# Routing a batch two batches behind instead of three, with its work at the end of the attention's steps

## What is computed

```
x = x + attn_a(layernorm(x), Mq, Mk, Mv)        # 8 heads, key size 64, value size 16
x = x + ffn(layernorm(x), w_gate, ...)          # 8 experts, hidden 512, one expert a token
x = x + attn_b(layernorm(x), wq, w_down, ...)   # 16 heads of 8, rotary, paged mask
x = x + ffn(layernorm(x), w_gate, ...)          # the same FFN again
```

```
probs = softmax(x @ w_gate + b_gate); route_p = max(probs); route_idx = argmax(probs)
y = relu(x @ W1[e] + b1[e]) @ W2[e] + b2[e]     # for e = route_idx of the token
out = y * route_p
```

## Time and profile before

| | before |
|---|---|
| median of three runs | 572.63 us |
| profiled execution | 575.24 us |
| its span | 573.4 us |
| mean granted clock | 0.857 |
| TensorE matmul busy | 423.3 us (74%) |
| VectorE busy | 324.9 us (57%) |
| ScalarE busy | 211.7 us (37%) |
| GpSimd busy | 202.3 us (35%) |
| the chain that ended last: TensorE, VectorE, issue | 56%, 15%, 8% |

### The profile page before, as it was taken

The page is one execution under the profiler, slowest core; times in us unless marked ns, Lnnn a source line. Parts: engine busy times, 40 slices in busy tenths (PEclk is TensorE's granted clock), DMA queues, the critical chain, the costliest instruction groups (busy, mean ns, idle before and its releaser), DMA issues.

```text
span 573.4 us, 14608 instructions
## 1 busy us (share of the span) xinstructions
PE 423.3 (74%) x4870; PEld 315.7 (55%) x4871; DVE 324.9 (57%) x1042; ACT 211.7 (37%) x483; POOL 202.3 (35%) x299
## 2 busy tenths in 40 slices
PE   2768878788872599955467899999888763999900
PEld 2646666666662377743135666766666652677800
DVE  2555656775666445426865576668776664444412
ACT  1445645544530022211135657655665400222200
POOL 3132335443445100027666335633612442000054
PEclk9968989998775699995567999999999955899965
DMA  8999200000000111111100000000000001111123
GB/s 271 348 337 296 83 2 13 11 5 5 10 11 27 29 55 53 50 38 37 27 0 2 1 2 3 0 0 0 1 2 10 29 19 32 39 53 54 41 70 90
DMA packets 40896, 30.91 MB, mean 54 GB/s; under 512 B 3344, under 2 KB 37008, under 8 KB 40592
## 3 DMA queue, kind: packets, MB, share of 16 engines
q1 hardware_dynamic: 32176, 23.06, 13.2%
q0 software_dynamic: 2048, 4.20, 2.5%
q10 hardware_dynamic: 6624, 3.02, 1.8%
HBM read 15.26 MB, written 15.01 MB: 53 GB/s over the span
## 4 chain that ended last, share of the span: by engine, by line
PE 56%; DVE 15%; issue 8%; POOL 7%; ACT 7%; DMA 4%; SPq 1%; ACTq 0%; DVEq 0%; POOLq 0%
PE S L1311 8%; PE bank L1324 7%; PE bank L1194 6%; POOL yg L1042 4%; PE S L1317 4%; PE S L1235 3%; PE S L1401 3%; ACT E L910 3%; PE bank L1354 3%; PE S L1402 2%; PE bank L1211 2%; DVE nmax L491 2%; PE bank L1414 2%; PE bank L1377 2%; PE bank L1154 2%
## 5 line engine op out<-in xcount | busy, mean ns | idle before, releaser
L829 ACT ACTIVATE E<-S,nmax 128x256 f32<-128x256 f32 x128 | 59.1, 478 | 59.7 <-DVE nmax L491 59.7
L1042 POOL DMA_INDIRECT yg<-slots,pos x32 | 30.8, 963 | 141.3 <-DMA slots<-yo 132.8
L872 ACT ACTIVATE hT<-S 128x512 f32<-128x512 f32 x46 | 27.5, 597 | 106.6 <-PE S L1317 106.6
L1003 POOL TENSOR_TENSOR vs<-Va,rden 128x512 f32<-128x512 f32 x32 | 33.3, 1040 | 80.1 <-DVE rden L520 77.2
L910 ACT ACTIVATE E<-S 128x1536 f32<-128x1536 f32 x32 | 46.4, 1450 | 25.7 <-PE S L1405 25.7
L1311 PE MATMUL S<-W,xgT 128*128 x92 | 52.3, 652 | 0.0
L677 DVE TENSOR_REDUCE nm<-bank 128x2 f32<-128x512 f32 x64 | 41.1, 684 | 16.1 <-PE bank L1377 16.1
L491 DVE TENSOR_REDUCE nmax<-S 128x4 f32<-128x1024 f32 x32 | 39.1, 1221 | 17.6 <-PE S L1235 16.6
L1324 PE MATMUL bank<-W,hT 128*128 x368 | 48.5, 276 | 0.0
L1324 PEld LDWEIGHTS bank<-W,hT 128*128 128x128 f32 x368 | 44.7, 192 | 0.1
L1148 PE MATMUL bank<-cst,xnb 128*128 128x128 f32 x44 | 11.9, 369 | 40.5 <-DVE xnb L415 29.6
(11 more groups left out here) (169 smaller groups left out, 1010.8 us busy)
## 6 DMA issues: line engine op xcount, KB each, us to landing
slots<-zeros SPq DMA_DIRECT2D x1, 8640.0 KB, 38.0
xg<-slots SPq DMA_DIRECT2D x46, 64.0 KB, 1.8
slots<-yo ACTq DMA_DIRECT2D x46, 64.0 KB, 1.6
W<-in_L_ffn_W SPq DMA_DIRECT2D x1, 2048.0 KB, 10.5
b<-in_L_ffn_b SPq DMA_DIRECT2D x1, 2048.0 KB, 20.1
x<-in_L_attn_a_x SPq DMA_DIRECT2D x4, 256.0 KB, 3.6
yg<-in_select SPq DMA_DIRECT2D x1, 1024.0 KB, 8.1
out<-x SPq DMA_DIRECT2D x8, 128.0 KB, 2.2
```

The lines of the kernel that those rows point to most:

```text
L829: last = act.activation(E[:, hp, h, c, :], S[hp % 2][:, h, c * T:(c + 1) * T], ACT.Exp, bias=nmax[:, hp, k:k + 1], accum_out=den[:, hp, k: ...
L1042: pool.indirect_dma_start(out=yg[:, t, :], out_offset=None, in_=xs_dram, in_offset=bass.IndirectOffsetOnAxis(pos[:, t:t + 1], 0)).then_inc ...
```

## The change

The router in the first attention runs one batch closer behind. Batch b now carries, of batch b-1, the statistics (step 2) and the norm's write, transpose and copy (step 3); of batch b-2, logits (step 0), ranks and places (step 1), and the scatter (step 2). On TensorE the router's instructions stand at the end of a step, behind projection and values. Batch 2 routes for the first time, so the gate's weights `wg` and `bg` count into a semaphore of their own group, waited for at batch 2. The tail is shorter by one batch and in another order. On GpSimd the zeroing of `keys` stands behind a wait for the expert table. In each FFN the first tile's product with W1 precedes the second tile's transpose.

```diff
@@ SyncE: loads
-            sp.dma_start(wg[:, :], wg_in).then_inc(w_loaded, 16)
-            sp.dma_start(bg[:, :], bg_in.unsqueeze(0).to_broadcast([P, NE])).then_inc(w_loaded, 16)
+            sp.dma_start(wg[:, :], wg_in).then_inc(b_loaded, 16)
+            sp.dma_start(bg[:, :], bg_in.unsqueeze(0).to_broadcast([P, NE])).then_inc(b_loaded, 16)
@@ VectorE: a_step
-                if hp == 0 and there(b - 3):
-                    route_logits(0, b - 3, 1 - p, pb[3])
-                if hp == 1:
-                    if there(b - 3): route_places(0, b - 3, 1 - p, pb[3])
-                if hp == 2:
-                    if there(b - 1): dve.wait_ge(a_x, b)
-                    if there(b - 2): norm_apply(1, b - 2, p)
-                    if there(b - 1):
-                        norm_stats(1, b - 1, 1 - p)
+                if hp == 0 and there(b - 2):
+                    route_logits(0, b - 2, p, pb[3])
+                if hp == 1 and there(b - 2):
+                    route_places(0, b - 2, p, pb[3])
+                if hp == 2 and there(b - 1):
+                    dve.wait_ge(a_x, b)
+                    dve.sem_inc(norm[1]["go"], 1)
+                    norm_stats(1, b - 1, 1 - p)
+                if hp == 3 and there(b - 1):
+                    norm_apply(1, b - 1, 1 - p)
@@ VectorE: tail
             a_recip(31, 3)
-            norm_apply(1, 6, 0)
             a_outT(30, 2)
-            route_logits(0, 5, 1, pb[3])
+            route_logits(0, 6, 0, pb[3])
             a_outT(31, 3)
-            route_places(0, 5, 1, pb[3])
             a_add(7, pb[0])
             dve.wait_ge(a_x, 8)
             norm_stats(1, 7, 1)
-            route_logits(0, 6, 0, pb[3])
+            route_places(0, 6, 0, pb[3])
             norm_apply(1, 7, 1)
-            route_places(0, 6, 0, pb[3])
             route_logits(0, 7, 1, pb[3])
             route_places(0, 7, 1, pb[3])
@@ ScalarE: a_step and tail
-                if hp == 3 and there(b - 2):
-                    norm_out(1, b - 2, p, pb[3])
+                if hp == 3 and there(b - 1):
+                    norm_out(1, b - 1, 1 - p, pb[3])
-            norm_out(1, 6, 0, pb[1])
@@ GpSimd: a_batch and tail
-                    if hp == 1 and there(b - 3):
-                        scatter(0, b - 3, 1 - p)
                     if hp == 2 and there(b - 1):
                         inverse_deviation(1, b - 1, 1 - p)
+                    if hp == (3 if isinstance(b, int) and b == 2 else 2) and there(b - 2):
+                        if isinstance(b, int) and b == 2:
+                            pool.wait_ge(slots_zero, 16)
+                        scatter(0, b - 2, p)
...
-            scatter(0, 5, 1)
             inverse_deviation(1, 7, 1)
             scatter(0, 6, 0)
             scatter(0, 7, 1)
+            pool.wait_ge(ffn[0]["table"], 1)
+            pool.memset(sofar[:, :], 0.0).then_inc(pool_const, 1)
             pool.wait_ge(a_scores, 4 * B)
             pool.memset(keys[:, :], 0.0).then_inc(bs["zero"], 1)
-            pool.wait_ge(ffn[0]["totals"], 1)
-            pool.memset(sofar[:, :], 0.0).then_inc(pool_const, 1)
@@ TensorE: a_step
                 last.then_inc(a_scores, 1)
-                if hp == 0 and there(b - 3): logits(0, b - 3, 1 - p, pb[3])
-                if hp == 1 and there(b - 3): ranks(0, b - 3, pb[3])
-                if hp == 3 and there(b - 2):
-                    pe.wait_ge(a_x, b)
-                    norm_transpose(1, b - 2, p, pb[3])
                 if nxt and hp < 3:
                     a_project(b + 1, 1 - p, hp, True)
                 if hp == 2 and lag:
-                    if there(b - 3):
-                        pe.wait_ge(ffn[0]["pos"], b - 2)
+                    if there(b - 2):
+                        pe.wait_ge(ffn[0]["pos"], b - 1)
...
                     a_values_out(g - 2, (hp + 2) % 4)
+                if hp == 0 and there(b - 2): logits(0, b - 2, p, pb[3])
+                if hp == 1 and there(b - 2): ranks(0, b - 2, pb[3])
+                if hp == 3 and there(b - 1):
+                    pe.wait_ge(a_x, b)
+                    norm_transpose(1, b - 1, 1 - p, pb[3])
@@ TensorE: tail
             a_values_out(30, 2)
-            logits(0, 5, 1, pb[3])
-            norm_transpose(1, 6, 0, pb[1])
+            logits(0, 6, 0, pb[3])
             pe.wait_ge(a_ot, 31)
             a_values_out(31, 3)
-            ranks(0, 5, pb[3])
             a_final(7, pb[0])
-            pe.wait_ge(ffn[0]["pos"], 6)
-            logits(0, 6, 0, pb[3])
             ranks(0, 6, pb[3])
-            pe.wait_ge(norm[1]["xnT"], 7)
             norm_transpose(1, 7, 1, pb[1])
@@ TensorE: ffn_tiles (fetch is the wait for tile s+1 and its transpose)
-                    if live(s + 1):
+                    first = isinstance(s, int) and s == 0
+                    if live(s + 1) and not first:
+                        fetch()
                     if live(s):
                         ...
+                    if first:
+                        fetch()
```

More of the change, by code:

```diff
@@ L535, in _ @@
             for b in range(3):
+                if b == 2:
+                    dve.wait_ge(b_loaded, 112)
                 for hp in range(4):
                     a_step(b, hp, b % 2, b > 0, True)
-            dve.wait_ge(w_loaded, 96)
+            dve.wait_ge(w_loaded, 64)
             with dve.Fori(0, 2) as h:
@@ L1016, in a_batch @@
                     a_values(b * 4 + hp, hp, p, lag)
-                    if hp == 1 and there(b - 3):
-                        scatter(0, b - 3, 1 - p)
                     if hp == 2 and there(b - 1):
                         inverse_deviation(1, b - 1, 1 - p)
+                    if hp == (3 if isinstance(b, int) and b == 2 else 2) and there(b - 2):
+                        if isinstance(b, int) and b == 2:
+                            pool.wait_ge(slots_zero, 16)
+                        scatter(0, b - 2, p)
             for b in range(3):
                 a_batch(b, b % 2, b > 0, True)
-            pool.wait_ge(slots_zero, 16)
             with pool.Fori(0, 2) as h:
@@ L1262, in _ @@
             for b in range(3):
+                if b == 2:
+                    pe.wait_ge(b_loaded, 112)
                 for hp in range(4):
                     a_step(b, hp, b % 2, b > 0, True)
-            pe.wait_ge(w_loaded, 96)
+            pe.wait_ge(w_loaded, 64)
             with pe.Fori(0, 2) as h:
@@ L1300, in step, with fetch @@
                         e = pe.value_load(expert[0:1, bass.ds(s, 1)], min_val=0, max_val=NE - 1)
-                    if live(s + 1):
+                    def fetch():
                         if isinstance(s, int):
@@ L1527, in b_router @@
                     what(router_at(b, point))
-            pe.wait_ge(b_loaded, 80)
+            pe.wait_ge(b_loaded, 112)
             pe.wait_ge(bs["const"], 3)
```

## The result

The changed kernel takes 588.8 us (median of four runs, 586.02 to 591.0), the one before 572.21 us (four, 571.34 to 573.14): 1.0275 times as long, 95% interval 1.023 to 1.032, or 16.6 us more. The prediction was 582.6 us, range 574 to 589. The profiled execution took 589.15 us, its span is 587.3, 13.9 us more than that of before.

The account below looks back on a forecast made before the run. The prediction saw the loop cycle as a relay between engines, not one full engine. Loop +2.2, batch 2 +2.6, batch 1 +4.0, batch 7 +0.3, tail -0.9 and -2.9, FFNs +0.6, clock +4.1: +10.0 on 572.63, 582.6 us, range 574 to 589.

Parts of the forecast that it names:

- Leg 4: From a batch's fourth maximum through the previous batch's norm write and transpose to the next scores: 5.0 us, 0.7 before.
- The cycle at full clock, 17.7 us: One loop batch replayed in four parts, 6.0 + 3.6 + 3.1 + 5.0 us, against 17.3 a batch before.
- leg 2: Second to third maximum of a batch: 3.6 us, 4.9 before, as ranks no longer hold the key projection.
- Batch 1's end +4.0: Batch 1 is the first behind which a norm is written: 5.0 us in place of 0.7, 0.3 less for the write.
- Batch 2, +2.6: Batch 2 now routes batch 0: 17.7 us in place of 15.1.
- The clock: TensorE falls to half clock behind each pause before batches 2 to 6: 1.5 us each, 7.5 less 3.4 before, +4.1.
- Batch 7 +0.3: Batch 7 loses the logits wait, gains the norm-write wait, and its last output waits for a scatter: +0.3, bounds -1.5 and +2.
- The tail -3.8: After batch 7: scatter no longer ahead of the last rstd, -0.9; zeroing no longer beside the expert table write, -2.9.
- The first product +0.3 an FFN: First product ahead of the second tile's transpose delays the second product: +0.3 us per FFN, bounds -0.5 and +0.6 each.
- Rival 1: The clock falls no more often than before: +5.9, 578.5 us; chance 0.22.
- Rival 2: Two slow stretches behind each idle, 3.0 us each instead of 1.5: 590.1 us; chance 0.10.
- Rivals 3 and 4: 3: pauses and their slow stretches go, 567.6 us, chance 0.13. 4: tail and loop cancel, 572.6 us, chance 0.05.

Follow-up runs that it names:

- the two kernels with the filled pause: The changed kernel with unread TensorE products before the norm's transpose: 18 products, 574.51 us; 10 products plus rstd computed before vs, 562.97 us.
- the filled kernel: The changed kernel with 18 unread products of constants on TensorE ahead of the norm's transpose in step 3: 574.51 us.
- the change with the old order: The changed kernel, but each FFN transposes its second tile before the first product, as before: 587.3 us.
- three_late: The kernel before, still three batches behind, with only TensorE's logits, ranks and norm transpose moved to the ends of their steps: 560.45 us.
- rstd first: The changed kernel, but GpSimd computes rstd of batch b-1 before vs of head pair 2 instead of behind it: 577.22 us.

## Why the prediction was right, and where it was short

The forecast was slower by 10.0 us; it is slower by 16.6, inside the range with 0.2 us to spare. The way and the mechanism came out as forecast; that the number stayed in the range is partly luck, since the clock's term alone was short by about 6 us, nearly all the room above the forecast. Point by point:

- **The waits before logits and ranks go: right.** 12.1 us before, 0.0 after.
- **Leg 4: right in every step.** Forecast 3.3 us from the fourth maximum to the norm's write, measured 3.57 (97.15 to 100.72); VectorE's wait for `rstd` forecast some 2 us, measured 2.0 to 2.1; the pause of TensorE forecast 4.1 us, measured 3.5 to 4.0. The write itself was priced 0.5 us too dear: 0.60 us for 1.1, with no tensor operation of GpSimd beside it. That this wait is a cause, the two kernels with the filled pause show at full clock: without it a batch is about 1.3 us shorter. It is not the whole of the leg: a batch is still 16.1 us then, against 14.7 three batches behind.
- **The cycle at full clock, 17.7 us:** the filled kernel shows 17.9, of which the filling is about 0.5. Right to 0.3. The sum of leg 2 is a little high, though (2.1 and 1.35 are 3.45, not 3.6), and the entry of the loop was priced too low: batch 3 takes 19.8 us in the filled kernel, 2 more than the others, where 0.3 was given for each end.
- **Batch 1's end +4.0:** +4.6, with the transpose already at half clock. Batch 2, +2.6 at full clock and a fall of the clock on top: +5.2, which is 2.6 and 2.6. The semaphore that batch 2 waits for counts seven loads, those of the second attention's weights with the gate's two, and cost nothing as forecast: the scores at 60.42 follow right behind the transpose.
- **The clock: the mechanism right, the size too small, and this is the term that was short.** "I take 1.5 each" was 2.4 to 2.8 us each in the rows of batches 2 to 6: 0.95 on the scores, 1.15 to 1.6 on the query projection, 0.25 on the transpose. I took a share of the 1.7 us of batch 3 and let another share fall into the idle; in the trace the clock is down some 2 us into the pause and stays down over the transpose, the scores and most or all of the query projection. Five falls at 2.65 us instead of 1.5 are 5.8 us more, against 6.6 missing. And there are six such pauses, not five, since batch 7 opens behind one too, where the half clock lasts longest (5.9 us by its rows); but the kernel before loses 4.6 in its own batch 7, so this adds little. The direct measure is the filled kernel: 14.3 us between it and the change, where the forecast had 7.5. Not all that the rows lose is on the path: in batch 3 it is 2.75 by the rows and 1.4 by the filled kernel, in batch 7 5.9 and 3.7.
- **Batch 7 +0.3:** -0.3, within its bounds. The scatter of batch 5 does stand ahead of the last `vs`, as forecast; TensorE's last values product waits 1.28 us for it.
- **The tail -3.8:** -3.4 from the residual add to the first tile. Of it the zeroing gave 2.6 (forecast 2.9): the wait behind it ended with the scatter's transfer, as forecast, and the zeroing stayed covered. The reading that the zeroing started first is not in the rows: `expert` stands at 184.01 and the zeroing at 184.35; what they show is that `expert` ends with it.
- **The first product +0.3 an FFN:** against the kernel before +0.1 in the first and +0.8 in the second, to the fourth tile's transpose; against the change with the old order +0.4 and +1.0. Right in sign, and short in the second.

Rival 1, a clock that falls no more often than before, is out by the windows (0.82 to 0.84 in each batch). Rival 2, 3.0 us a pause and 590.1 in all, was nearer in size (588.8), but its reason, two slow stretches behind each pause, is not what happened: each batch has one. Only batch 7, from which it argued, has a stretch over several steps. Rivals 3 and 4 are out. What was not seen at all is that the two halves of the change, the place in the step and the one batch less of slack, have opposite signs. The first alone gains 10 us. The second was not run alone; the 28.3 us between three_late (560.45) and the change hold it, with the new tail, the zeroing and the first product, which by their traces are 2 to 3 us the other way.

What stays open: no run gives what the clock's falls cost in the kernel before; a filling of its pause before the logits would write to the PSUM bank that ScalarE reads at that time, and was not tried. The gain of the late place, 10.1 us, holds both shorter waits and fewer falls. Its traces split it in part: batches 4 and 5, at full clock in both kernels, are 5.7 us shorter together, which is waits alone; in batches 6 and 7 both change.

## What to carry to other kernels

Work moved closer to its producer should be followed to the last link of its chain, here a two-element `rstd` on a third engine that sits behind a product it has nothing to do with: one wait of 3.7 us a batch took the place of two short ones, 2.0 and 1.0. Ask for each half of such a change what it does alone; moving consumers behind independent work gained 10 us, and the rest of the change, the shorter slack above all, lost more than that. And price a pause of TensorE by what runs right behind it: here the work behind a pause of 3.5 to 4.0 us took 2.4 to 2.8 us longer at half clock, and 5.9 in the last batch; with the pauses filled 14.3 us came back.

## What the hardware showed that was not expected

- All six pauses of 3.5 to 4.0 us in the batches of the changed kernel that open with scores were followed by a stretch at half clock. Of the six pauses of 2.2 to 2.8 us in the profiled execution with rstd first, five were followed by one and one was not, and those of 2.80 us went one each way; the four runs of that kernel spread over 12 us. The Trainium skill, "TensorE: Matmul & The Clock Gate", section "HAM oscillation — how this bites in real kernels", says that such gaps bring the half clock back in each iteration; the six agree.
- Products of constants that nobody reads kept the clock at 1.00 over five batches, and the kernel took 14.3 us less.
- VectorE's `expert`, 0.31 us in the change, took 3.95 us beside a GpSimd zeroing of 3.52 us and ended with it (187.96 and 187.87). After the move VectorE's reciprocal at 199.59 ran its normal 0.25 us beside the zeroing. The Trainium skill, "SBUF — State Buffer", section "SBUF: two separate sides", gives the shared pair to whichever starts first, against some VectorE operations only. The rows agree that one was blocked for the whole zeroing and another not; which of the two started first they do not show. Whether a later zeroing would hold up the first tile's copy, as the prediction drew from the rule, no run tests: the copy always starts about 1 us behind the zeroing's end (188.63 and 187.69, 203.97 and 202.98).
- The norm's write of two 128x128 tiles took 0.60 us without a tensor operation on GpSimd, and 1.44 us beside `vs`.
